# Two units weighed together every second step, and the image's value rows by DMA, in the attention of a recurrent stack

## The reference, cut to what matters

```python
def _L3_cond_ref(word, image, attention_mask, c_attn_w, ...):
    q_word, k_word, v_word = jnp.split(word @ c_attn_w + c_attn_b, 3, axis=-1)
    img = image[:, None, :]
    k = jnp.concatenate([img @ uk_w.T + uk_b, k_word], axis=1)
    v = jnp.concatenate([img @ uv_w.T + uv_b, v_word], axis=1)
    ...
    scores = jnp.where(causal, q @ k.T / sqrt(32), -10000.0) + mask
    out = jax.nn.softmax(scores) @ v
    return out.reshape(B, S, 512) @ c_proj_w + c_proj_b
x = x + _L0(x, cond, ...); x = x + _L1(x, cond, ...); x = x + _L2(x, cond, ...)
x = x + _L3_cond_ref(x, cond, mask, ...)
```

## Time and profile before

| | before |
|---|---|
| median of 3 runs | 3827.79 us |
| the profiled execution: time, span | 3826.17 us, 3824.5 us |
| PE busy | 3746.8 us (98%) |
| DVE, ACT, POOL busy | 2358.2 (62%), 1104.8 (29%), 39.6 us (1%) |
| mean granted clock of PE | 0.998 |
| DMA | 47.18 MB, 12 GB/s |

### The profile page before, as it was taken

The page is one execution under the profiler, slowest core; times in us unless marked ns, Lnnn a source line. Parts: engine busy times, 40 slices in busy tenths (PEclk is TensorE's granted clock), DMA queues, the critical chain, the costliest instruction groups (busy, mean ns, idle before and its releaser), DMA issues. The chain is left out here.

```text
span 3824.5 us, 170528 instructions
## 1 busy us (share of the span) xinstructions
PE 3746.8 (98%) x77565; PEld 2492.1 (65%) x77565; DVE 2358.2 (62%) x8897; ACT 1104.8 (29%) x3969; POOL 39.6 (1%) x192
## 2 busy tenths in 40 slices
PE   7999999999999999999999999999998999999998
PEld 5777676766677767676667776767654555555555
DVE  3566666666666666666666666666645666666665
ACT  2211111111111111111111111111115665665565
POOL 0000000000000000000000000000000000000000
PEclk9999999999999999999999999999999999999999
DMA  4100000000000000000000000000010000000000
GB/s 172 36 4 4 3 4 3 4 3 3 4 3 4 3 4 3 3 4 3 4 3 3 3 4 4 3 4 3 36 38 4 12 10 12 15 13 15 12 7 20
DMA packets 34547, 47.18 MB, mean 12 GB/s; under 512 B 5856, under 2 KB 22288, under 8 KB 33824
## 3 DMA queue, kind: packets, MB, share of 16 engines
q1 hardware_dynamic: 31520, 29.96, 2.5%
q10 hardware_dynamic: 2304, 6.29, 0.4%
HBM read 27.86 MB, written 8.39 MB: 9 GB/s over the span
## 5 line engine op out<-in xcount | busy, mean ns | idle before, releaser
L253 PE MATMUL bank<-wh,h 128*16 128x256 f32 (+1 forms) x16960 | 982.6, 372 | 7.6 <-ACT h L352 6.9
L231 PE MATMUL bank<-wh,states 128*8 128x256 f32 x16352 | 976.1, 379 | 9.4 <-DVE states L481 9.4
L253 PEld LDWEIGHTS bank<-wh,h 128*16 128x16 f32 (+1 forms) x16960 | 487.0, 96 | 321.6 <-ACT h L352 25.1
L231 PEld LDWEIGHTS bank<-wh,states 128*8 128x8 f32 x16352 | 445.1, 90 | 346.1 <-DVE states L481 20.5
L453 DVE STREAM_TRANSPOSE tp<-bank 128x256 f32<-128x256 f32 x512 | 230.7, 451 | 605.2 <-PE bank L231 603.8
L237 PE MATMUL bank<-wh,states 128*8 128x128 f32 x16352 | 540.0, 273 | 0.0
L237 PEld LDWEIGHTS bank<-wh,states 128*8 128x8 f32 x16352 | 447.2, 90 | 108.1
L357 ACT ACTIVATE gates_sb<-pre_sb 128x32 f32<-128x32 f32 x512 | 117.5, 229 | 1207.9 <-DVE pre_sb L455 1207.9
L272 PE MATMUL bank<-probs_extra,w_qkv 128*32 128x128 f32 x11904 | 393.1, 273 | 0.0
L272 PEld LDWEIGHTS bank<-probs_extra,w_qkv 128*32 128x32 f32 x11904 | 339.9, 110 | 64.3
L352 ACT ACTIVATE h<-sum 128x64 f32<-128x64 f32 (+1 forms) x530 | 135.1, 255 | 775.0 <-DVE sum L405 775.0
(11 more groups left out here) (142 smaller groups left out, 3462.4 us busy)
## 6 DMA issues: line engine op xcount, KB each, us to landing
rows<-in_x_dram SPq DMA_DIRECT2D x32, 256.0 KB, 2.9
out_dram<-X SPq DMA_DIRECT2D x32, 256.0 KB, 2.6
w_qkv<-in_L_cond_c_attn_w_dram SPq DMA_DIRECT2D x1, 3072.0 KB, 11.4
w_qkv<-in_L_cond_w_W_dram ACTq DMA_DIRECT2D x4, 512.0 KB, 7.8
wh<-in_L_cond_w_W_dram ACTq DMA_DIRECT2D x4, 512.0 KB, 13.9
wx<-in_L_cond_Wx_dram SPq DMA_DIRECT2D x2, 1024.0 KB, 7.3
wh<-in_L_cond_Wh_dram SPq DMA_DIRECT2D x2, 1024.0 KB, 9.6
wx<-in_mask_Bx1x1xS_ff_dram SPq DMA_DIRECT2D x8, 256.0 KB, 3.2
```

Of the source, the lines that this page charges most:

```text
L231: mm = pe.matmul(mem.ps0[32 * j:32 * j + B, 0:2 * P], state[:, k, :], columns_of(mem.wh0[:, k, 0:3:2, :], j), start=(k == 0), stop=(k == K ...
L253: mm = pe.matmul(mem.ps12[32 * j:32 * j + B * len(ls), P * l0:P * l1], h12[:, k, (n - 1) % HR, l0:l1, :].rearrange("p l b -> p (l b)"), co ...
```

## The change

It has three parts.

1. In a step with i even, PE does `weigh(i - 4)` and `weigh(i - 3)` one after the other at the step's end, and in an odd step it weighs nothing. `probsT` gets a buffer for qc = 0, one for qc = 2, and one that qc = 1 and 3 share; ACT's wait before an even unit is for unit v - 4 and not v - 2.
2. The product with `pick` (L823) goes, and `pick` with its POOL work early in the scan. The extras are laid out anew: rows 0 to 3 of each 32 partitions of `v_extra` are the later keys' of the four heads, rows 4 to 7 the image's. DVE keeps the rows of the later keys by three instructions of 4 x 512, one for each qc below 3 (partitions 0, 32 and 64 on). The image's rows come by four DMAs a user from `v_rows`, inside the core's memory, issued on SP's queue: for users 0 and 1 at the start of the attention, after POOL has zeroed `v_extra` there, and for user u + 2 behind the output transfers of user u. DVE's keep of `hidden` and a user's first `weigh` wait for them.
3. For that `v_rows` holds the image's rows four times, at partitions 0, 32, 64 and 96 on: `image_v` does four products in place of one in each of its steps (8 columns each, in the four column tiles), DVE adds the bias in four instructions over four steps of the scan, and the bias is loaded to 128 partitions and not 8.

```diff
@@ scan, PE, DVE @@
             def image_v(k):
                 pe.wait_ge(s.turn_kept, 2 * KC)
-                mm = pe.matmul(mem.xps[0][0:B, :], mem.condT[:, k, :], mem.image_T[:, k, :], ...)
+                for q in range(QC):
+                    mm = pe.matmul(mem.xps[0][FAR * q:FAR * q + B, :], mem.condT[:, k, :], mem.image_T[:, k, :], ...)
...
-                for _, k in tail_of(n - 1, "image"):
-                    if k == KC - 1:
-                        ...
-                        nc.vector.tensor_tensor(mem.v_rows[0:B, :], mem.xps[0][0:B, :], mem.v_rows[0:B, :], ALU.add)
+                q = n - IMAGE_KEPT
+                if 0 <= q < QC:
+                    dve.wait_ge(s.image_made, 1)
+                    dve.wait_ge(s.image_bias_in, 16)
+                    rows = slice(FAR * q, FAR * q + B)
+                    nc.vector.tensor_tensor(mem.v_rows[rows, :], mem.xps[0][rows, :], mem.v_rows[rows, :], ALU.add)
@@ attention, SP @@
+            def load_image_rows(u):
+                if u >= 2:
+                    sp.wait_ge(s.weighed, PER * (u - 1))
+                for g in range(HPG):
+                    dst = mem.v_extra[HPG + g:HPG + g + FAR * (QC - 1) + 1:FAR, u % 2, :].rearrange("p (h x) -> p h x", h=HG)
+                    src = mem.v_rows[u:u + FAR * (QC - 1) + 1:FAR, :].rearrange("p (h x) -> p h x", h=HG)
+                    sp.dma_start(dst[:, :, HD * g:HD * (g + 1)],
+                                 src[:, :, HD * g:HD * (g + 1)]).then_inc(s.image_rows_in[u % 2], 16)
             load_mask(1)
+            sp.wait_ge(s.extra_zero, 1)
+            load_image_rows(0)
+            load_image_rows(1)
             for u in range(B):
                 ...
+                if u + 2 < B:
+                    load_image_rows(u + 2)
@@ attention, PE @@
                     pe.wait_ge(s.hidden_ready, u + 1)
-                    pe.matmul(bank[:, :], mem.pick[:, u, :], mem.v_rows[:, :], start=True, stop=False)
...
                     if v % PER == 0:
                         pe.wait_ge(s.product_kept, place[u, "hidden", 0] + 1)
+                        pe.wait_ge(s.image_rows_in[u % 2], 16 * HPG * (u // 2 + 1))
...
-                if i >= 3:
+                if i >= 4 and i % 2 == 0:
+                    weigh(i - 4)
                     weigh(i - 3)
@@ attention, ACT @@
-                if first == 0 and v >= 2:
-                    act.wait_ge(s.weighed, v - 1)
+                if first == 0 and v >= 4 - 2 * (qc % 2):
+                    act.wait_ge(s.weighed, v - 1 if qc % 2 else v - 3)
@@ attention, DVE @@
                 elif kind == "hidden":
-                    ins = nc.vector.tensor_tensor(mem.v_extra[:, u % 2, :]..., bank[:, :]...,
-                                                  mem.head_block[:, :].unsqueeze(1).to_broadcast([P, HG, P]), ALU.mult)
+                    dve.wait_ge(s.image_rows_in[u % 2], 16 * HPG * (u // 2 + 1))
+                    for q in range(QC - 1):
+                        rows = slice(FAR * q, FAR * q + HPG)
+                        ins = nc.vector.tensor_tensor(mem.v_extra[rows, u % 2, :]..., bank[rows, :]...,
+                                                      mem.head_block[rows, :].unsqueeze(1).to_broadcast([HPG, HG, P]), ALU.mult)
@@ attention, POOL @@
+            nc.gpsimd.memset(mem.v_extra[:, :, :], 0.0).then_inc(s.extra_zero, 1)
@@ memory @@
-        mem.probsT = [sb(ctx, f"probsT{q}", [P, HPG * P * (3 + q)]) for q in range(2)]
+        odd = sb(ctx, "probsT_odd", [P, HPG * P * QC])
+        mem.probsT = [rows[:, 2, :], odd, sb(ctx, "probsT2", [P, HPG * P * 3]), odd]
```

More of the change, by code:

```diff
@@ L117 @@
 TAIL = tail_plan()
+IMAGE_KEPT = 1 + max(n for n in TAIL if ("image", KC - 1) in TAIL[n])
 def counts(per_step):
@@ L318, in image_v @@
                 pe.wait_ge(s.turn_kept, 2 * KC)
-                mm = pe.matmul(mem.xps[0][0:B, :], mem.condT[:, k, :], mem.image_T[:, k, :],
-                               start=(k == 0), stop=(k == KC - 1))
+                for q in range(QC):
+                    mm = pe.matmul(mem.xps[0][FAR * q:FAR * q + B, :], mem.condT[:, k, :], mem.image_T[:, k, :],
+                                   start=(k == 0), stop=(k == KC - 1))
                 if k == KC - 1:
@@ L540, in _ @@
                                     pattern=[[-1, P]], channel_multiplier=1).then_inc(s.drop_made, 1)
[L541 to L552, removed]
             pool.wait_ge(s.fill_done, nfill[last0])
@@ L912, in weigh @@
                         mm = pe.matmul(mem.banks[7][HD * g:HD * (g + 1), cols], mem.v[:, u % 2, kc, at:at + HD],
-                                       mem.probsT[v % 2][:, x * P:(x + 1) * P], start=False, stop=(kc == qc),
+                                       mem.probsT[qc][:, x * P:(x + 1) * P], start=False, stop=(kc == qc),
                                        skip_group_check=True)
@@ L950, in exps @@
                     act.wait_ge(s.image_in, i // QC + 1)
-                nc.scalar.activation(mem.extras[:, slot, 0:EXTRAS * HPG:EXTRAS], mem.neg_max[:, slot, :], ACT.Exp,
+                nc.scalar.activation(mem.extras[:, slot, 0:HPG], mem.neg_max[:, slot, :], ACT.Exp,
                                      bias=mem.later_max[:, u % 2, qc:qc + 1])
@@ L967, in keep_turn @@
                     if r <= qc:
-                        nc.scalar.copy(mem.probsT[v % 2][:, HPG * r * P:HPG * (r + 1) * P],
+                        nc.scalar.copy(mem.probsT[qc][:, HPG * r * P:HPG * (r + 1) * P],
                                        bank[:, :]).then_inc(s.turn_kept, 1)
@@ L1022, in keep @@
                 elif kind == "hidden":
-                    ins = nc.vector.tensor_tensor(mem.v_extra[:, u % 2, :].rearrange("p (h c) -> p h c", h=HG),
-                                                  bank[:, :].rearrange("p (h c) -> p h c", h=HG),
-                                                  mem.head_block[:, :].unsqueeze(1).to_broadcast([P, HG, P]), ALU.mult)
+                    dve.wait_ge(s.image_rows_in[u % 2], 16 * HPG * (u // 2 + 1))
+                    for q in range(QC - 1):
+                        rows = slice(FAR * q, FAR * q + HPG)
+                        ins = nc.vector.tensor_tensor(mem.v_extra[rows, u % 2, :].rearrange("p (h c) -> p h c", h=HG),
+                                                      bank[rows, :].rearrange("p (h c) -> p h c", h=HG),
+                                                      mem.head_block[rows, :].unsqueeze(1).to_broadcast([HPG, HG, P]), ALU.mult)
                 elif kind == "rows":
@@ L1198, in __init__ @@
         self.extras_in = new("extras_in")
-        self.picked = new("picked")
+        self.extra_zero = new("extra_zero")
+        self.image_rows_in = [new(f"image_rows_in{q}") for q in range(2)]
         self.hidden_ready = new("hidden_ready")
```

19 lines of the change are left out of this document (8 added, 11 removed).

## The result

| | median, us | runs | profiled execution | its span |
|---|---|---|---|---|
| before | 3828.10 | 22 (3824.63 to 3830.23) | 3826.17 | 3824.5 |
| changed | 3833.45 | 22 (3830.72 to 3835.2) | 3834.24 | 3832.5 |

The ratio is 1.0013, with a 95% interval of 1.0007 to 1.0019: +5.35 us, small but beyond its interval. The time lies in the range given (3819.5 to 3833.5), by luck: it got there by waits and by a loss in user 0 that the prediction does not have, while the drops of the clock that it counted did not come. The forecast of -0.9 us had the wrong sign, and the -6.0 us without the clock did not come.

The account below looks back on a forecast made before the run. PE's instruction sequence was taken to bound users 1 to 7. Pairs -7.4, hidden rows +2.0, user 0 -0.6 and clock +5.1 gave -0.9 us: 3825.3 profiled, 3826.9 median, range 3819.5 to 3833.5.

Parts of the forecast that it names:

- the -6.0 us without the clock: Whole kernel: pairs -7.4, hidden rows +2.0, user 0 -0.6 us, before any drop of the clock.
- The bound, and the seams: PE in users 1 to 7: its instruction sequence is the time; each pair saves 0.14 us, 7.4 in all.
- The three keeps: DVE's keep of hidden, users 1 to 7: two more instructions cost 1.38 us per user; net of pick, 2.0 more.
- The product with `pick`, put at 1.1: PE, once per user: removing these two instructions saves 1.1 us.
- Part 3 and the DMAs: Scan and image-row transfers: extra products, bias instructions and DMAs cost 0, with 0 to 0.5 us as range for the scan.
- a move of over 0.5 us: Sign of being wrong: a stage up to 2882 us that moves by over 0.5 us.
- the cover of the moved weighing: Ahead of even steps' scores: at qc = 0, 0.58 us of cover goes, and the remaining slack holds.
- 0.69 and 0.22 are left: Steps into qc = 0: slack in us left before PE waits for ACT's last exponential and for the fifth transpose's bank.
- In the other direction nothing tightens: Steps with two weighings: they give ACT and DVE more time, so no new wait was counted.
- The cover was needed: Rival, steps into qc = 0: late ACT idles PE up to 0.58 us in 27 head groups, up to 15.7; chance 0.04.
- User 0: User 0 and the step into user 1: 0.6 us less, range 0 to 2.2, from pick and pairs.
- The clock: Pause after hidden, users 1 to 7: at 2.33 us, three of seven followed by a drop, 1.7 each, 5.1 more.

Follow-up runs that it names:

- e5: Changed kernel with sums ahead of the keep of rows at l = 5 and 9, and one keep of hidden with the image's DMAs behind it: 3812.78 us.
- e8: Changed kernel with sums ahead of the keep of rows, one keep of hidden, and the old rhythm of one weighing per step: 3817.51 us.
- e2: Changed kernel with the old rhythm of one weighing per step; three keeps and image rows by DMA stay: 3829.39 us.
- e3: Changed kernel with DVE's sums and reciprocals ahead of its keep of rows in steps l = 5 and 9: 3831.95 us.
- e6: Changed kernel with the old rhythm of weighings in user 0 alone, pairs from there on: 3832.82 us.
- e12: Changed kernel with a fourth keep of hidden, of four rows of zeros that nothing needs: 3844.43 us.
- e9: Changed kernel with PE's two weighings at l = 2 and 6 put ahead of rows, in the pause: 3817.82 us.
- e11: e3 with PE's pause at l = 2 of users 1 to 7 filled with eight products that nothing uses: 3821.86 us.
- e4: Changed kernel with one keep of hidden, 128 x 512, and the image rows' DMAs issued behind it: 3821.47 us.

## Why the prediction was wrong

- **The bound, and the seams: right.** PE's order of instructions is the time; 0.14 per pair is what e5 against e8 shows.
- **The three keeps: right for users 1 to 7.** 1.38 more, a pause of 2.17; e2 gives 0.24 per user for the whole part, where 0.28 was forecast. The product with `pick`, put at 1.1, was worth 1.15 (step l = 2 takes 8.28 before and 7.13 in e8).
- **Part 3 and the DMAs: nothing that shows.** The attention starts at 2881.40 instead of 2882.34. I had named a move of over 0.5 us as a sign of being wrong, but in the profiles of the eleven experiments, which all have part 3, it starts anywhere from 2881.16 to 2882.50. The first scores come 0.28 later even so, as the first eight products of the attention take 6.59 us instead of 5.37, at a clock of 0.78 from 2882 to 2894 (before: 0.86).
- **The step that failed: the cover of the moved weighing, with "0.69 and 0.22 are left" and "In the other direction nothing tightens".** I checked it for the weighing of qc = 0 alone, against ACT's exponentials and banks, and there it did hold: the steps l = 4, 8, 12 and 0 came as worked out. For qc = 2 I took over the 0.14 "as only the seams differ" and put the cover at nothing, without listing the other waits of the steps l = 2, 6, 10 and 14. At l = 6 and 10 the shares come from DVE, behind a keep; the cover was 1.01 us and 0.35 was to spare. It cost 2 x 0.69 x 7 = 9.7 us, more than the pairs' 7.4. "The cover was needed" was a rival with a chance of 0.04, but on another engine and in other steps.
- **User 0: -0.6 forecast, +4.7 measured** (3.31, and 1.4 in the step behind it). The pick's 1.1 us came at l = 2 (5.20 instead of 6.34) and went again at l = 3 (4.31 instead of 3.35), in the wait for shares behind the three keeps; I had counted the keeps only where `rows` follows them. The rest goes with three drops of the clock, which my clock term did not consider in user 0. They come with the pairs, and why is open.
- **The clock: the mechanism right, the count not.** Three drops behind the pause were forecast and none stands in the changed kernel's profile, which was named as a sign of being wrong; five, two and three of seven in e3, e6 and e12, each 1.6 to 1.8 us, as sized from the earlier trace rows. Which users get one is not settled. The timed runs give only a mean clock, 0.995 to 0.997 in the changed kernel's 22, where its profile has 0.996.
- **The sum** for the profiled execution: +0.3 ahead of the attention's scores, +4.7 for user 0, +4.1 for users 1 to 7 up to l = 11 (six times 0.54, and 0.84; that is 9.7 of waits and 1.7 of keeps less 7.2 of seams, 0.136 each), and -1.0 at the end. These make the 8.1 that was measured. In the median it is 5.35; the profiled executions lie 1.9 below and 0.8 above theirs. The profile before is one of the better executions: of 33 runs of that kernel beside e2 to e6, 18 had a clock of 0.998 like it and took 3827.0 on average, the other 15 had 0.995 to 0.997 and took 3829.4.

## What to carry to other kernels

Before work is moved from the end of a step, list every wait of the following step, on each engine that feeds it, with the time by which its releaser is early; the smallest of them, not the one that comes to mind, says what may be moved. Cheap independent work belongs in the longest pause: here two weighings moved there are worth 16 us (e9 against the changed kernel), and where a pause is followed by the lower clock it pays a second time (e11 against e3). An instruction on DVE that was split by partitions cost its full time for each part (three times 0.69 us for once), and where the next thing behind it is awaited, as the shares in user 0, that counts there too.

## What the runs showed of the hardware that I had not expected

- A pause of 2.17 us amid dense work is followed by the lower level in some users and not in others of the same execution (in none of seven in the profiles of the changed kernel and e2, five in e3, two in e6), at 1.6 to 1.7 us each; in the profiles of e4 and e11, where it is 0.79 and 0.39, none was.
- A change elsewhere, as in e3 and e6, moves where these drops fall, so that 9.7 us won on PE's path can show as 1 us in the median.
